# Attention output moved out of the score banks into spare columns of the turned probabilities' banks

## The chip, the cores and the metric

The kernel runs on one core of one Trainium2 chip. The metric is the device time of one execution in microseconds. Before the change it is 995.27 us, the median of three runs (992.34 to 995.49).

## What is computed

One transformer block with adaptive layer norm, on 8 batches of 512 tokens of width 256. Cut to what matters here, with `h` the modulated layer norm of `x`:

```python
# light attention: windows of 64 tokens, each sees itself and its two neighbours, 8 heads of 64
q, k, v = split(layernorm(h) @ wqkv_l)
sim = einsum('bhnid,bhnjd->bhnij', qw * scale, kk)      # kk, vv: three windows side by side
lo = einsum('bhnij,bhnjd->bhnid', softmax(sim), vv);  light_out = lo @ wo_l
# heavy attention: 256 tokens chosen by a routing score as queries, 256 as keys
ho = einsum('bhij,bhjd->bhid', softmax(hq * scale @ hk), hv);  heavy_out.at[iq].set(ho @ wo_h)
x = x + ga * (light_out + heavy_out)
# MLP: y = square(relu(n(x) @ W_fc.T)) @ W_proj.T, then five steps of a spiking neuron on y
x = x + gb * spikes(y) / 5
```

## The kernel before

Five instruction streams are written out by hand, one for each engine (TensorE, VectorE, ScalarE, GpSimd, SyncE), and are tied together by counting semaphores. What an engine does comes in the order in which its stream issues it. There is no scheduler.

Attention is cut into 24 slots for each batch, which make one iteration: 16 light ones (`LIGHT`; a pair of heads p and a tile of 128 queries m) and 8 heavy ones. There are 8 iterations: `first`, six of `loop`, and `last`. The running number of a slot is n. The work of three slots lies side by side in each slot:

- TensorE, slot n: `scores(n + 2)`, the units of the slot (projections, MLP, transposes, listed in `SLOT_UNITS`), `turn(n)` (transposes the probabilities into `ps_pT`), `attend(n - 1)` (the products with v, into `ps_oT`).
- VectorE, slot n: `copy_out(n - 2)` (adds the two parts of the output and stores them in `loT` or `hoT`, the latter inside `late`), `invert(n + 1)` (reciprocal of the row sums), `minimum(n + 2)` (row minimum of the scores), then its part of the units and of the stages (layer norm, router comparisons, neuron).
- ScalarE, slot n: `copy_pT(n - 1)` (copies the turned probabilities to `probsT`), `exp_step(n + 2)`, its part of the units, `normalize(n + 1)`.

Scores hold negative products, so the minimum is what softmax needs as maximum. The scores lie in two PSUM banks (`ps_scores`, at most 256 of 512 columns each), and the output of attention lies in columns 256 to 383 of the same two banks. The turned probabilities lie in two others (`ps_turned`, columns 0 to 255). Columns 256 to 511 of those are unused. The other four banks hold the MLP's sums and the units' results. No two engines may touch one bank at a time, so each stream waits by bank:

- `scores(n + 1)` waits for `exp_ready` of slot n.
- `attend(n - 1)` waits for `copy_pT(n - 1)`, for `copy_out(n - 2)` and for `exp_step(n + 2)`, for the latter with `pe.wait_ge(exp_ready, min(n + 4, SLOTS * B))` (L1062; its n is the slot attended to).
- `copy_out(n - 2)` waits for the end of `attend(n - 2)` and for the end of `scores(n + 2)` (L1321).
- `turn(n)` waits for `normalize(n)` and for `copy_pT(n - 1)`.

Units named below: HT (slots 0 and 2) transposes routed rows, which ScalarE and VectorE store as `hT`; V (slot 0), HV (slots 3, 7), NV (slots 20, 22, 23) are value projections, copied by VectorE; HO (slot 1) multiplies the last heavy outputs with `wo_heavy`, and waits for the copy_out of the last heavy slot, done in slot 1; Z3 (slot 7) transposes the third norm; FC and YA (slots 8 to 16) are the MLP; ZT (slots 15, 16) and RK (slots 13, 16) are a transpose (drained by ScalarE as `full`) and the ranks from the router comparisons; HQ and HK of slot 17 project routed queries and keys; LO (slots 18 to 21) is the light output projection.

Of the kernel before, what the change touches and what calls it, by code (L numbers as in the profile page):

```python
# [33 lines left out]
P = 128  # L34
B, N, D = 8, 512, 256
H, DH = 8, 64
INNER = H * DH
W = 64
SEL = 256
# [11 lines left out]
SLOTS = LIGHT + HEAVY  # L51
# [130 lines left out]
def score_columns(s, part):  # L182

    if s >= LIGHT:
        return 0, SEL
    m = s % T
    return (W if m == 0 and part == 0 else 0), (2 * W if m == T - 1 and part == 1 else 3 * W)
# [9 lines left out]
def probs_buffer(s):  # L197

    return s % T if s < LIGHT else (1, 2, T)[(s - LIGHT) % 3]


def adaln_block_kernel(nc, x, gamma_h, wq_h, wkv_h, wo_h, ln_g, ln_b, wqkv_l, wo_l, rt_q, rt_kv,
                       w_fc, w_proj, c, wmod, out):
    with ExitStack() as ctx:
        def sb(name, shape, dt=F32):
            return ctx.enter_context(nc.sbuf_tensor(name, shape, dt))

        def sem(name):
            return ctx.enter_context(nc.semaphore(name))
# [48 lines left out]
        v = sb("v", [P, T, INNER])  # L258
        v_r = sb("v_r", [P, SEL // P, INNER])
# [47 lines left out]
        gates_sign = probsT[0:B, :]  # L307

        ps_scores = ctx.enter_context(nc.psum_tensor("ps_scores", [P, 2, 512], F32))
        ps_oT = ps_scores[:, :, SEL:SEL + P]  # L310
        ps_turned = ctx.enter_context(nc.psum_tensor("ps_turned", [P, 2, 512], F32))
        ps_pT = ps_turned[:, :, 0:SEL]
        ps_y = [ctx.enter_context(nc.psum_tensor(f"ps_y{i}", [P, 512], F32)) for i in range(2)]
        ps_unit = [ctx.enter_context(nc.psum_tensor(f"ps_unit{i}", [P, 512], F32)) for i in range(BANKS)]

# [23 lines left out]
        scores_ready = sem("scores_ready")  # L339
        min_ready = sem("min_ready")  # L340
        exp_ready = sem("exp_ready")
# [3 lines left out]
        pT_copied = sem("pT_copied")  # L345
        oT_ready = sem("oT_ready")
        oT_copied = sem("oT_copied")
# [48 lines left out]
        def wait_drained(eng, segment, b, *units):  # L396

            last = {}
            for u in sorted(units, key=BANKED[segment].index):
                bank, before = bank_use(segment, b, u)  # L400
                last[bank] = before + 1
            for bank, count in last.items():
                eng.wait_ge(drained[bank], count)
# [478 lines left out]
        def _(pe):  # L882
# [160 lines left out]
            def turn(n, s):  # L1043


                pe.wait_ge(probs_ready, n + 1)
                if not (isinstance(n, int) and n == 0):
                    pe.wait_ge(pT_copied, n)
                for i in range(3 if s < LIGHT else 4):
                    for c in range(2):  # L1050
                        run = (i - 1) % 3 if s < LIGHT else i ^ 2 * c
                        rows = slice(c * W, (c + 1) * W)
                        ins = pe.transpose(ps_pT[:, c, i * W:(i + 1) * W],  # L1053
                                           probs[rows, probs_buffer(s), run * P:(run + 1) * P], ident[rows, rows])
                ins.then_inc(pT_ready, 1)

            def attend(segment, b, n, s):

                pe.wait_ge(pT_copied, n + 1)
                if n > 0:  # L1060
                    pe.wait_ge(oT_copied, n)
                pe.wait_ge(exp_ready, min(n + 4, SLOTS * B))  # L1062

                halves = [slice(i * W, (i + 1) * W) for i in range(2)]
                if s < LIGHT:
                    p, m = divmod(s, T)
                    if p == 0 and m == 2:
                        wait_drained(pe, segment, b, ("V", 3))
                    turned = probsT[:, 0:6 * W].rearrange("p (i c n) -> p i c n", i=3, c=2)
                    cols = [slice(p * P + h * DH, p * P + (h + 1) * DH) for h in range(2)]  # L1070
                    for g, h in ((0, 0), (1, 1), (1, 0), (0, 1)):
                        both = probsT[halves[g], h * W:h * W + 2 * (3 - 2 * h) * W].rearrange(
                            "p (w n) -> p w n", w=2)[:, :, 0:W]
                        ins = pe.matmul(ps_oT[halves[h], g ^ h, :], v[halves[g], m, cols[h]], both,  # L1074
                                        start=True, stop=m == (T - 1, 0)[g])
                    for g, h in ((0, 0), (1, 1), (1, 0), (0, 1)):
                        if m != (T - 1, 0)[g]:
                            w = 1 - g
                            ins = pe.matmul(ps_oT[halves[h], g ^ h, w * W:(w + 1) * W], v[halves[g], m + 1 - 2 * g, cols[h]],  # L1079
                                            turned[halves[g], 2, h ^ w, :], start=False, stop=True)  # L1080
                else:
                    p, _ = divmod(s - LIGHT, SEL // P)
                    if s == LIGHT:
                        wait_drained(pe, segment, b, ("HV", 0), ("HV", 1))
                    turned = probsT[:, :].rearrange("p (c i n) -> p i c n", c=2, i=4)
                    cols = [slice(p * P + h * DH, p * P + (h + 1) * DH) for h in range(2)]
                    for t in range(2):
                        for g, h in ((0, 0), (1, 1), (1, 0), (0, 1)):
                            ins = pe.matmul(ps_oT[halves[h], g ^ h, :], v_r[halves[g], t, cols[h]],  # L1089
                                            turned[halves[g], 2 * h + t, :, :], start=(t == 0), stop=(t == 1))  # L1090
                ins.then_inc(oT_ready, 1)

# [18 lines left out]
            for k in range(KD):  # L1111
                ins = pe.transpose(ps[:, k * B:(k + 1) * B], silu[:, 2, k * P:(k + 1) * P], ident[0:B, 0:B])
# [4 lines left out]
            for k in range(KD):  # L1117
                ins = pe.matmul(ps[:, :], silu_first[:, k, :], raw_wmod[k][:, 0:512], start=(k == 0), stop=(k == KD - 1))
# [3 lines left out]
            for q in range(4):  # L1122
                for k in range(KD):
                    ins = pe.matmul(ps[:, q * B:(q + 1) * B], raw_wmod[k][:, 3 * D + q * P:3 * D + (q + 1) * P],
                                    siluT[:, k, :], start=(k == 0), stop=(k == KD - 1))
            ins.then_inc(full_bank, 1)
            for i in range(3):
                ps, full_bank = fill("setup", 0, ("MR", i))
                for k in range(KD):
                    ins = pe.matmul(ps[0:B, :], siluT[:, k, :], raw_wmod[k][:, i * 512:(i + 1) * 512],  # L1130
                                    start=(k == 0), stop=(k == KD - 1))
# [19 lines left out]
        def _(dve):  # L1151
# [150 lines left out]
            def minimum(n, s):  # L1302
                dve.wait_ge(scores_ready, n + 1)
                (lo, hi), other = score_columns(s, 0), score_columns(s, 1)
                if (lo, hi) == other:
                    ins = dve.tensor_reduce(row_min[:, s % 3, :], ps_scores[:, :, lo:hi], AX.X, ALU.min)  # L1306
                else:
                    dve.tensor_reduce(row_min[:, s % 3, 0:1], ps_scores[:, 0, lo:hi], AX.X, ALU.min)
                    lo, hi = other
                    ins = dve.tensor_reduce(row_min[:, s % 3, 1:2], ps_scores[:, 1, lo:hi], AX.X,  # L1310
                                            ALU.min)
                ins.then_inc(min_ready, 1)
# [5 lines left out]
            def copy_out(n, s):  # L1318

                dve.wait_ge(oT_ready, n + 1)  # L1320
                dve.wait_ge(scores_ready, min(n + 5, SLOTS * B))  # L1321
                dst, (p, m) = (loT, divmod(s, T)) if s < LIGHT else (hoT, divmod(s - LIGHT, SEL // P))
                dve.tensor_reduce(dst[:, p, m * P:(m + 1) * P], ps_oT.rearrange("p g n -> p n g"), AX.X,  # L1323
                                  ALU.add).then_inc(oT_copied, 1)
# [79 lines left out]
            def iteration(segment, b, first=False, last=False):  # L1404
                for s in range(SLOTS):
                    n = SLOTS * b + s
                    if first and s in (2, 3):
                        routed_weights(s - 2)
                    if not (first and s < 2):
                        copy_out(n - 2, (s - 2) % SLOTS)  # L1410
                    if not (last and s + 1 >= SLOTS):
                        invert(n + 1, (s + 1) % SLOTS)
                    if not (last and s + 2 >= SLOTS):
                        minimum(n + 2, (s + 2) % SLOTS)
                    if not last and s == 7:
                        stats2(b + 1)
                    for u in slot_units(s, first, last):
                        unit(segment, b, u)
                    stages(segment, b, s, first, last)
# [29 lines left out]
            cols = ps[:, 0:4 * B].rearrange("p (q b) -> p q b", q=4)  # L1449
# [40 lines left out]
            for b in range(1, B - 1):  # L1490
                iteration("loop", b)
# [47 lines left out]
```

## Time and profile before

| | |
|---|---|
| median of the runs | 995.27 us (992.34 to 995.49) |
| profiled execution, its own time | 1000.88 us |
| its span | 999.1 us |
| TensorE busy | 855.5 us, 86% |
| TensorE weight loads busy | 654.3 us, 65% |
| VectorE busy | 556.6 us, 56% |
| ScalarE busy | 583.5 us, 58% |
| GpSimd busy | 396.5 us, 40% |
| mean granted TensorE clock | 0.93 |
| chain that ended last | TensorE 59%, VectorE 22%, ScalarE 8%, issue 6% |

The rows come from the profiled execution, the median from runs without a profile. Busy shares are means over the whole span; an engine may be the limit in one stretch and idle in another. Times in rows are us from the span's start. One loop iteration lasts about 112.5 us. The one read closest starts at about 501.9. The granted clock is given as a share of TensorE's full 2.4 GHz.

### The profile page before, as it was taken

The page shows a single profiled execution, that of the slowest core. Times are in us where ns is not written, and L with a number is a line of the kernel's source. Part 1 is how long each engine was busy: PE and PEld are TensorE (multiplying, and loading weights), DVE is VectorE, ACT ScalarE, POOL GpSimd, SP SyncE. Part 2 cuts the span into 40 slices and gives each one's busy share as a digit, 9 for nine tenths or more (in the row PEclk, how much of TensorE's full clock was granted, in tenths as well). Part 3 has the DMA queues.
Part 4 walks back from the last instruction along what each step waited for, and adds up shares of the span by engine and source line. Part 5 has one row for each costly group of instructions (what it writes and reads, how often), then busy time and mean ns, then how long its engine had stood idle before and what let it go on. Part 6 is the DMA issues. An engine that isn't in the chain of part 4 may idle for free.

```text
span 999.1 us, 23412 instructions
## 1 busy us (share of the span) xinstructions
PE 855.5 (86%) x8914; PEld 654.3 (65%) x8914; DVE 556.6 (56%) x1602; ACT 583.5 (58%) x1682; POOL 396.5 (40%) x437
## 2 busy tenths in 40 slices
PE   5758599799988999799988999799988999899655
PEld 2436466577756876577756876577756876587455
DVE  7645634764557554764557554764557554614344
ACT  1156556576656765676656765576556765676332
POOL 3322031375424542365424543365424542252243
PEclk9878779999999999999999999999999999999768
DMA  8220002100210012200220012200220011200100
GB/s 314 67 80 2 27 28 70 59 2 23 80 59 23 2 38 85 59 2 19 71 73 23 1 39 85 60 2 17 72 73 22 3 38 54 59 2 2 37 22 22
DMA packets 32479, 45.33 MB, mean 45 GB/s; under 512 B 3928, under 2 KB 26720, under 8 KB 32368
## 3 DMA queue, kind: packets, MB, share of 16 engines
q1 hardware_dynamic: 26944, 31.24, 9.8%
q0 software_dynamic: 4608, 12.59, 3.8%
q8 instruction: 72, 1.18, 0.5%
q14 instruction: 39, 0.32, 0.1%
q10 hardware_dynamic: 816, 0.00, 0.0%
HBM read 28.85 MB, written 14.97 MB: 44 GB/s over the span
## 4 chain that ended last, share of the span: by engine, by line
PE 59%; DVE 22%; ACT 8%; issue 6%; DMA 2%; POOL 2%; SPq 0%; DVEq 0%; POOLq 0%; ACTq 0%
PE ps_unit L895 25%; PE ps_y L1006 7%; PE ps_unit L943 6%; ACT probs L829 5%; PE ps_unit L948 4%; PE ps_turned L1053 4%; PE ps_scores L1089 3%; PE ps_scores L1074 3%; DVE row_min L1306 3%; PE ps_scores L1038 3%; PE ps_scores L1029 3%; DVE loT L1323 2%; ACT hT L794 1%; DVE bn L1268 1%; DMA late<-in_L_wmod 1%
## 5 line engine op out<-in xcount | busy, mean ns | idle before, releaser
L829 ACT ACTIVATE probs<-ps_scores,row_min 128x192 f32<-128x192 f32 (+2 forms) x384 | 161.3, 425 | 182.8 <-DVE row_min L1306 125.6
L839 ACT ACTIVATE probs<-probs,row_inv 128x192 f32<-128x192 f32 (+2 forms) x384 | 155.7, 458 | 0.0
L1323 DVE TENSOR_REDUCE loT<-ps_scores 128x128 f32<-128x256 f32 x128 | 53.5, 418 | 141.3 <-PE ps_scores L1029 92.0
L895 PE MATMUL ps_unit<-xT,wfcT 128*128 128x512 f32 (+1 forms) x432 | 112.8, 404 | 9.4 <-DVE xT L1247 8.8
L895 PE MATMUL ps_unit<-xT,wqkv 128*128 128x512 f32 x384 | 109.6, 422 | 3.3 <-POOL xT L653 3.3
L1006 PEld LDWEIGHTS ps_y<-wprojT,hid_parts 128*128 128x128 f32 x768 | 99.3, 190 | 9.9 <-issue 6.0
L432 POOL TENSOR_TENSOR hid<-hid 128x512 f32<-128x512 f32 (+1 forms) x64 | 63.5, 992 | 106.4 <-ACT hid L807 105.1
L1006 PE MATMUL ps_y<-wprojT,hid_parts 128*128 128x256 f32 x768 | 104.6, 284 | 0.2
L895 PEld LDWEIGHTS ps_unit<-xT,wfcT 128*128 128x128 f32 x432 | 78.6, 206 | 33.4 <-issue 20.2
L578 POOL TENSOR_SCALAR veps<-mv 128x4 f32<-128x4 f32 (+1 forms) x25 | 5.1, 202 | 227.7 <-DVE mv L1166 133.1
L1074 PE MATMUL ps_scores<-probsT,v 64*64 64x128 f32 x1024 | 58.7, 299 | 38.9 <-ACT probs L829 38.6
L1053 PEld LDWEIGHTS ps_turned<-ident,probs 64*128 64x128 f32 x1280 | 55.6, 140 | 54.9 <-issue 44.3
L895 PEld LDWEIGHTS ps_unit<-xT,wqkv 128*128 128x128 f32 x384 | 71.3, 193 | 24.3 <-issue 10.2
L436 POOL TENSOR_TENSOR hid_parts<-hid,hid_parts 128x512 fp32r<-128x512 f32 (+1 forms) x64 | 79.2, 1237 | 13.4 <-ACT hid_parts L811 11.2
L1053 PE MATMUL ps_turned<-ident,probs 64*128 64x64 f32 x1280 | 82.2, 241 | 1.9 <-ACT probsT L851 1.7
L619 POOL DMA_INDIRECT sorted_rows<-hn,rank x64 | 64.4, 1006 | 45.7 <-DVE rank L1350 33.0
L847 ACT ACTIVATE probsT<-ps_turned 128x384 f32<-128x384 f32 x128 | 61.9, 484 | 33.6 <-PE ps_scores L1079 33.3
L1306 DVE TENSOR_REDUCE row_min<-ps_scores 128x2 f32<-128x512 f32 (+1 forms) x128 | 77.1, 602 | 2.5 <-PE ps_scores L1029 2.5
L1323 DVE TENSOR_REDUCE late<-ps_scores 128x128 f32<-128x256 f32 x64 | 27.0, 422 | 88.0 <-PE ps_scores L1038 44.8
L829 ACT ACTIVATION_READ_ACCUMULATOR probs<-ps_scores,row_min 128x1 f32 x384 | 75.3, 196 | 0.0
L1029 PE MATMUL ps_scores<-kT,qT 64*64 64x192 f32 (+1 forms) x1024 | 71.8, 317 | 3.3 <-ACT probs L829 3.3
L943 PE MATMUL ps_unit<-wo_light,loT 128*128 128x256 f32 x256 | 63.8, 392 | 0.0
(158 smaller groups left out, 1690.9 us busy)
## 6 DMA issues: line engine op xcount, KB each, us to landing
xa<-in_L_attn_x SPq DMA_DIRECT2D x8, 512.0 KB, 5.0
routed<-sorted_rows SPq DMA_DIRECT2D x16, 256.0 KB, 3.0
lx<-in_L_attn_x SPq DMA_DIRECT2D x8, 512.0 KB, 3.8
out_x<-spikes SPq DMA_DIRECT2D x16, 256.0 KB, 3.0
routed_out<-late SPq DMA_DIRECT2D x8, 256.0 KB, 2.1
full<-mod_rows SPq DMA_DIRECT2D x7, 256.0 KB, 5.0
sorted_rows<-hn,rank POOLq DMA_INDIRECT x64, 2.4
gate_a<-mod_rows SPq DMA_DIRECT2D x8, 128.0 KB, 3.5
```

What stands on the lines that cost most here:

```text
L436: eng.tensor_tensor(hid_parts[1][:, i % 2, cols], square, hid_parts[0][:, i % 2, cols].bitcast(F32), ALU.subtract).then_inc(low, 1)
L619: pool.indirect_dma_start(out=sorted_rows[r], out_offset=bass.IndirectOffsetOnAxis(ap=rank[:, r, t:t + 1], axis=0), in_=hn[:, t, :], in_of ...
L829: ins = act.activation(probs[:, probs_buffer(s), probs_columns(s, part)], ps_scores[:, part, lo:hi], ACT.Exp, bias=row_min[:, s % 3, part: ...
L839: ins = act.activation(rows, rows, ACT.Identity, scale=row_inv[:, s % 3, part:part + 1])
L895: ins = pe.matmul(ps, w(wi, k, w_cols), a(ai, k, a_cols), start=(n == 0), stop=(n == 3 * KD - 1))
L943: ins = pe.matmul(ps[:, 0:D], loT[:, p, i * P:(i + 1) * P], wo_light[:, p, :], start=(p == 0), stop=(p == PAIRS - 1))
L1006: ins = pe.matmul(ps_y[t // 2][:, (t % 2) * D:(t % 2 + 1) * D], hid_parts[hi][:, i % 2, t * P:(t + 1) * P], wprojT[wi][:, f, :], start=(f ...
L1029: ins = pe.matmul(ps_scores[c * W:(c + 1) * W, w, lo:hi], qT[heads[h], p % 2, query:query + W], kT[heads[h], p % 2, first_key + lo:first_k ...
L1053: ins = pe.transpose(ps_pT[:, c, i * W:(i + 1) * W], probs[rows, probs_buffer(s), run * P:(run + 1) * P], ident[rows, rows])
L1074: ins = pe.matmul(ps_oT[halves[h], g ^ h, :], v[halves[g], m, cols[h]], both, start=True, stop=m == (T - 1, 0)[g])
L1306: ins = dve.tensor_reduce(row_min[:, s % 3, :], ps_scores[:, :, lo:hi], AX.X, ALU.min)
L1323: dve.tensor_reduce(dst[:, p, m * P:(m + 1) * P], ps_oT.rearrange("p g n -> p n g"), AX.X, ALU.add).then_inc(oT_copied, 1)
```

## The change

The output tile `ps_oT` moves from `ps_scores` to the spare columns of `ps_turned`. Since turn writes bank c from the row half c, the products of the output now go to the bank of their row half g, in place of g ^ h. attend no longer waits for the exponential. turn waits for the copy_out of two slots before, whose bank it writes. copy_out waits for the copy of the turned probabilities, which reads the same banks, in place of the scores, and VectorE issues it behind the inverse and the minimum instead of ahead of them.

```diff
-        ps_oT = ps_scores[:, :, SEL:SEL + P]
         ps_turned = ctx.enter_context(nc.psum_tensor("ps_turned", [P, 2, 512], F32))
         ps_pT = ps_turned[:, :, 0:SEL]
+        ps_oT = ps_turned[:, :, SEL:SEL + P]
...
                 pe.wait_ge(probs_ready, n + 1)
-                if not (isinstance(n, int) and n == 0):
+                if n > 0:
                     pe.wait_ge(pT_copied, n)
+                if n > 1:
+                    pe.wait_ge(oT_copied, n - 1)
...
                 pe.wait_ge(pT_copied, n + 1)
                 if n > 0:
                     pe.wait_ge(oT_copied, n)
-                pe.wait_ge(exp_ready, min(n + 4, SLOTS * B))
...
-                        ins = pe.matmul(ps_oT[halves[h], g ^ h, :], v[halves[g], m, cols[h]], both,
+                        ins = pe.matmul(ps_oT[halves[h], g, :], v[halves[g], m, cols[h]], both,
                                         start=True, stop=m == (T - 1, 0)[g])
...
-                            ins = pe.matmul(ps_oT[halves[h], g ^ h, w * W:(w + 1) * W], v[halves[g], m + 1 - 2 * g, cols[h]],
+                            ins = pe.matmul(ps_oT[halves[h], g, w * W:(w + 1) * W], v[halves[g], m + 1 - 2 * g, cols[h]],
...
-                            ins = pe.matmul(ps_oT[halves[h], g ^ h, :], v_r[halves[g], t, cols[h]],
+                            ins = pe.matmul(ps_oT[halves[h], g, :], v_r[halves[g], t, cols[h]],
...
                 dve.wait_ge(oT_ready, n + 1)
-                dve.wait_ge(scores_ready, min(n + 5, SLOTS * B))
+                dve.wait_ge(pT_copied, min(n + 2, SLOTS * B))
...
-                    if not (first and s < 2):
-                        copy_out(n - 2, (s - 2) % SLOTS)
                     if not (last and s + 1 >= SLOTS):
                         invert(n + 1, (s + 1) % SLOTS)
                     if not (last and s + 2 >= SLOTS):
                         minimum(n + 2, (s + 2) % SLOTS)
+                    if not (first and s < 2):
+                        copy_out(n - 2, (s - 2) % SLOTS)
```

## Rows read from the trace of the kernel before

**Rows 1.** Waits of the whole span: who waited for whom, total us, times, longest us.
```profile
ACT probs L829 <- DVE row_min L1306: 125.6, 128, 2.8
ACT probs L829 <- DVE row_min L1310: 57.1, 57, 2.7
PE ps_scores L1074 <- ACT probs L829: 38.6, 47, 2.1
```
**Rows 2.** Timeline, slot 4: start, length, engine, line, operation, idle time before and its releaser.
```profile
522.35 0.41 DVE L1323 TENSOR_REDUCE loT<-ps_scores 128x128 f32<-128x256 f32 x1
522.68 0.15 DVE L1316 RECIPROCAL row_inv<-row_sum 128x2 f32<-128x2 f32 x1
522.75 0.53 DVE L1306 TENSOR_REDUCE row_min<-ps_scores 128x2 f32<-128x384 f32 x1
...
522.89 0.40 PE L1053 MATMUL ps_turned<-ident,probs 64*128 64x64 f32 x6
523.21 1.66 DVE L1186 SCALAR_TENSOR_TENSOR h<-xa,rstd,full 128x256 f32<-128x256 f32 x4
...
524.38 0.45 PE L1074 MATMUL ps_scores<-probsT,v 64*64 64x128 f32 x8 [1.09 <-ACT probs L829]
```
**Rows 3.** Timeline of TensorE, slot 7: an output and the scores behind it.
```profile
536.69 0.45 PE L1074 MATMUL ps_scores<-probsT,v 64*64 64x128 f32 x8
...
537.07 0.51 PE L1029 MATMUL ps_scores<-kT,qT 64*64 64x192 f32 x8
```
**Rows 4.** Timeline, slot 1: the copy of the last heavy output, and HO.
```profile
506.74 0.42 DVE L1323 TENSOR_REDUCE late<-ps_scores 128x128 f32<-128x256 f32 x1
...
507.30 5.38 PE L948 MATMUL ps_unit<-wo_heavy,late 128*128 128x256 f32 x16 [1.59 <-DVE late L1323]
```
**Rows 5.** Timeline, slot 23: copy, turn, and the heavy output.
```profile
612.04 0.42 DVE L1323 TENSOR_REDUCE late<-ps_scores 128x128 f32<-128x256 f32 x1 [2.12 <-PE ps_scores L1029]
...
613.43 0.46 PE L1053 MATMUL ps_turned<-ident,probs 64*128 64x64 f32 x8
...
614.09 0.67 PE L1089 MATMUL ps_scores<-probsT,v_r 64*64 64x128 f32 x16 [0.19 <-ACT probs L829]
```
**Rows 6.** Timelines of TensorE and VectorE: HV in slot 3, the copy in slot 5.
```profile
518.47 1.66 PE L895 MATMUL ps_unit<-wkv_r,hT 128*128 128x512 f32 x6 [0.72 <-DVE hT L1342]
```
```profile
525.40 0.42 DVE L1323 TENSOR_REDUCE loT<-ps_scores 128x128 f32<-128x256 f32 x1 [0.53 <-PE ps_scores L1029]
```
**Rows 7.** Timelines, slots 15 and 16: cast, copy, RK and output.
```profile
576.59 0.43 DVE L1244 CAST xT<-full 128x512 fp32r<-128x512 f32 x1 [1.75 <-ACT full L764]
...
579.42 0.41 DVE L1323 TENSOR_REDUCE loT<-ps_scores 128x128 f32<-128x256 f32 x1
```
```profile
579.64 0.24 PE L980 MATMUL ps_unit<-ones_bf,late 128*128 128x1 bf16 x4 [0.55 <-DVE late L1234]
...
581.69 0.45 PE L1074 MATMUL ps_scores<-probsT,v 64*64 64x128 f32 x8 [1.02 <-ACT probs L829]
```
**Rows 8.** Waits inside the first iteration, then inside the last one.
```profile
PE ps_scores L1074 <- ACT probs L829: 10.9, 12, 2.1
```
```profile
PE ps_scores L1074 <- ACT probs L829: 2.4, 5, 1.1
...
PE ps_scores L1089 <- ACT probs L829: 1.6, 2, 0.8
```
**Rows 9.** Stretches: bounds, length, busy us of PE, PEld, DVE, ACT, POOL, clock, DMA.
```profile
528.00:532.00 4.00, 2.89 (x43) 1.88 (x36) 3.06 (x14) 2.48 (x10) 1.23 (x2) 1.00 0.38 131
578.50:582.50 4.00, 2.43 (x54) 1.82 (x52) 2.24 (x8) 1.97 (x6) 1.05 (x1) 1.00 0.09 33
582.60:586.00 3.40, 3.40 (x19) 3.39 (x17) 2.51 (x7) 2.33 (x8) 2.70 (x3) 0.51 0.08 25
```
**Rows 10.** Timeline of TensorE: HO and FC of iteration 1, FC of iteration 4.
```profile
172.45 3.69 PE L948 MATMUL ps_unit<-wo_heavy,late 128*128 128x256 f32 x16 [1.57 <-DVE late L1323]
...
202.03 3.03 PE L895 MATMUL ps_unit<-xT,wfcT 128*128 128x512 f32 x12 [1.00 <-DVE xT L1247]
...
538.58 4.44 PE L895 MATMUL ps_unit<-xT,wfcT 128*128 128x512 f32 x12 [1.00 <-DVE xT L1247]
```

## Prediction

> **What bounds the kernel now.** I read the page first. TensorE is busy for 86% of the span, VectorE for 56%, ScalarE for 58%, and two thirds of the chain that ended last is TensorE's. So time can only come from TensorE's idle time, or from TensorE running at the wrong clock.
>
> The list of waits comes second [rows 1]. ScalarE's exponentials wait for the row minimum 128 + 57 times, that is in practically every slot, about 1 us each. The exponential therefore starts when the minimum ends, not when ScalarE comes free. TensorE's largest single wait is the one in front of the attention output: 38.6 us in 47 places, all for the exponential. It is the line `pe.wait_ge(exp_ready, min(n + 4, ...))` in attend, there because the output lies in the score banks that the exponential is still reading. Heavy slots wait little.
>
> Third I read one slot in order of time [rows 2]. It is slot 4. VectorE comes free late at F = 522.35 (its centering of the next batch ran until then), copies the output of two slots ago (L1323), and only then takes the minimum (start 522.75, next VectorE instruction 523.21). TensorE has finished turning the probabilities (522.89 + 0.40 = 523.29) and stands for 1.09 us until the attention output can start at 524.38. The scores of the next slot come 0.38 us behind such an output [rows 3].
>
> Last I read the granted clock in stretches. It is 1.00 nearly everywhere in the loop, except for three stretches of about 3.4 us in nearly every loop iteration at about half, the lower level of 1.2 GHz: in HO (slot 1), in the first FC units (slot 8) and in HQ/HK (slot 17).
>
> **The change, part by part.** TensorE's operations, their number and their order stay; so do VectorE's but for copy_out, which goes from before the inverse and the minimum to behind them. No DMA moves, and SP's and POOL's queues are untouched. A wait in attend (for the exponential) goes, one in turn (for copy_out) comes, copy_out waits for the copy of the turned probabilities instead of the scores.
>
> *(a) The minimum no longer stands behind the copy.* L1323 delays the next VectorE instruction by 0.33 us (start to start, 522.35 to 522.68, where the inverse begins [rows 2]). Minimum, exponential and all that ScalarE does behind it come 0.33 us earlier where ScalarE waits for the minimum, which is nearly always [rows 1].
>
> *(b) The output no longer waits for the exponential.* The next wait is that of the next scores, which still need the exponential. The output's 0.38 us [rows 3] go under that wait. (a) and (b) together can give 0.33 + 0.38 = 0.71 us per long wait, and a short wait whole.
>
> *(c) The new wait.* turn now waits for copy_out, which stands behind inverse and minimum. From F: 0.07 (inverse) + 0.46 (minimum, 522.75 to 523.21) + 0.42 (copy) + about 0.12 hand-over. The last is an estimate from [rows 4], where the copy ends at 507.16 and TensorE's HO follows at 507.30. So turn starts no earlier than F + 1.07, output F + 1.47, next scores F + 1.85. Behind turn on TensorE's queue stand the output and these scores. Before, the scores came at 524.38 + 0.38 = F + 2.41. A slot with a long wait thus gives 0.56 us, a slot with a short one (w below 0.56) gives w. In slots without a wait the copy is in time. The tightest one that I found is slot 23 [rows 5]: copy ready at 612.04 + 1.07 = 613.11, turn at 613.43, 0.32 us spare. From below (the copy takes turn's whole gain) a slot gives 0, from above 0.71.
>
> *(d) Slot by slot through one loop iteration* (waits for the exponential in slots 2, 4, 5, 6, 16, 23).
> Slot 23: the wait of 0.19 goes [rows 5]: 0.18.
> Slot 1: HO needs the copy of the last heavy output [rows 4]. The copy comes 0.53 later behind inverse and minimum. The chain before it (exponential of slot 0, hT, the copy of V) comes 0.33 earlier. That costs 0.20 us, hidden by nothing: TensorE stands for 1.59 us already.
> Slots 2 and 3: HV waits for hT, which ScalarE makes behind the exponential [rows 6]: 0.33 earlier, by (a), whatever attend does.
> Slots 4 to 8: slot 4 would give 0.56. But VectorE sat idle only 0.53 before slot 5's copy [rows 6]; from there to FC in slot 8 it works nearly without a stop, so slots 5 and 6 pass nothing more on (FC waits for its last product). 0.53.
> Slots 15 and 16: RK waits 0.55 for the comparisons, these for a cast, this for ScalarE's `full` behind the exponential [rows 7]: 0.33 earlier. Then slot 16's own 0.71, less a few hundredths because turn waits for the copy: 0.67.
> Sum 0.18 - 0.20 + 0.33 + 0.53 + 1.00 = 1.84 us per iteration, 11.0 us in the six loop iterations. The first iteration has 12 waits with 10.9 us [rows 8], nine of them over 0.56: at most 5.6 us; I take 4, since some of these slots are paced by VectorE's weight parts. The last one has 4.0 us in 7 waits [rows 8] and the HO loss; capped at 0.56 each I take 2.5. Waits: 17.5 us.
>
> *(e) The clock.* In the 4 us before HQ, TensorE was busy for 2.43 us at full clock, then the clock fell for 3.4 us [rows 9]. In a like stretch around slot 6 it was busy for 2.89 us and the clock stayed. The change takes 1.0 us of idle time out of exactly the first stretch, and leaves it busier than the second. I expect this fall to go, six times. Price of one: HO took 5.38 us with one [rows 4] and 3.69 without [rows 10], 1.69; FC 4.44 against 3.03 [rows 10], 1.41; in HQ, 3.40 us all busy at 0.51 are 1.67 us lost [rows 9]. I take 1.6, so 9.5 us. The falls in HO and FC stand behind waits that the change doesn't shorten; I leave them in, and put their going in the range.
>
> By the Trainium skill (TensorE: Matmul & The Clock Gate, Part 1) the clock falls after an idle stretch and comes back after a busy one. Here it fell after stretches that were mostly busy by the trace, so the trace agrees in direction only. Read as idle alone, no wait of 1 us would matter, no fall would go, and the sum would be that of the second rival.
>
> *(f) Banks of the output's products.* The output now goes to bank g (the half of the rows that are contracted) instead of g ^ h. Sixteen heavy records of 128 columns take 0.67 us [rows 5], 0.042 each; a whole-array record of 256 columns takes 3.69/16 = 0.231 [rows 10], 0.115 for 128. Two to three run at a time already, two row halves on one bank included. I take 0; bounds are 0 and half the output's time, -0.19 us in each of 192 slots, -36 us.
>
> The Trainium skill (TensorEngine Tiling (Array Packing), Restrictions and Gotchas) says that different row tiles can't access the same bank at once. If they were held apart now, the new placing would free them, which gives the fourth rival. The overlap just worked out speaks against it.
>
> **Sum.** Against the profiled execution's own 1000.88 us: 1000.88 - 17.5 - 9.5 = 973.9, a ratio of 0.973. The median of the runs is 995.27, so 968.4 us.
>
> **Rivals.**
> 1. *More falls of the clock go.* With each iteration shorter, HO and FC meet other states of the clock; the second iteration already shows HO at 3.69 and FC at 3.03. All would give 6 x 1.69 + 5 x 1.41 = 17.2 more: 956.7, or 951.3 at the median. Against it: the waits before HO and FC remain. 0.22, mostly part of it.
> 2. *Only the waits go; HQ's fall stays.* 1000.88 - 17.5 = 983.4, at the median 977.9. For it: 2.43 and 2.89 of 4 us lie near one another. 0.17.
> 3. *turn takes over the wait.* If the hand-over from minimum to copy to turn costs 0.5 us more than I take, (c) gives nothing, and only the 0.33 of HV and of RK remain: about 4 us, 991. 0.06. For it: in slot 4 the new wait is 0.53 us, near to what it replaces.
> 4. *The output's products run faster.* Up to 36 us beyond the forecast; half of that gives 950. 0.03.
> 5. *Slower: new falls.* Slots 2 to 7 run at full clock now, with four waits. Idle time there moves together, to in front of turn (0.5 us) and of the scores. If this makes the clock fall, each fall costs 1.6 us. It decides from 17 falls on (27/1.6), three in each iteration; two in each together with HQ's fall staying make it even. At four in each it is about 1007 (24 x 1.6 = 38.4 lost against 27.0 gained). 0.06.
> The forecast itself has 0.42, and 0.04 is left for what I don't see.
>
> **Numbers.** 968.4 us. Its own range is 962 to 974. The whole range goes up to rival 2 with some weakening (982) and down to nearly all falls gone (952). This leaves rivals 3 to 5 and the rest outside, about 0.19. A difference under 0.3% (3 us) can't be told from no change. Faster by more: 0.42 + 0.22 + 0.17 + 0.03 and two thirds of rival 3, 0.88. Within 0.3%: 0.05. Slower: 0.07.
>
> **What the profile after would show.** The wait of the output for the exponential is gone from the list of waits. In its place stand the scores' wait for the exponential, and turn's for loT/late, in slots 4, 6 and 16, together about half of the old 41 us. The exponential starts about 0.1 us after the minimum as now, but 0.33 us earlier behind the scores. HO's wait is about 1.8 us instead of 1.59. The clock is 1.00 in the HQ units, 12 of them in 1.69 us. An iteration of the loop takes about 3.4 us less. The forecast is wrong if turn's wait sums to more than 20 us, if the HQ units still take 2.9 us (too low by 9), or if HO and FC run at full clock (too high by up to 17).

## The result and the profile after

The changed kernel takes 967.97 us (median of four executions, 965.52 to 968.22) against 995.38 us. The ratio is 0.971, 95% interval 0.966 to 0.976. In the profiled execution the span is 966.3 us where it was 999.1. The profiled execution of before lay 5.5 us above its median, so of these 32.8 us some five are chance. The spread of executions below goes largely, but not wholly, with the granted clock. Ratios leave out an execution that lies over 1.5% above the shortest one of its kernel; here that is one of the first experiment's six.

The list of waits of the changed kernel (total us, times, longest us; answers to [rows 1] and, for HO, to [rows 4]):

```profile
ACT probs L829 <- DVE row_min L1307: 79.0, 99, 2.5
...
ACT probs L829 <- DVE row_min L1311: 34.9, 27, 2.5
...
PE ps_turned L1055 <- DVE loT L1324: 18.6, 28, 1.4
...
PE ps_unit L948 <- DVE late L1324: 12.2, 8, 1.7
...
DVE late L1324 <- ACT probsT L851: 6.4, 3, 2.7
DVE loT L1324 <- ACT probsT L847: 6.2, 15, 0.7
...
PE ps_scores L1029 <- ACT probs L829: 3.7, 3, 1.7
...
PE ps_turned L1055 <- DVE late L1324: 3.4, 4, 1.5
```

The output's wait for the exponential (38.6 us) is gone. turn's wait for the copy has come, 22.0 us. ScalarE's wait for the minimum went from 182.7 to 113.9 us: the minimum comes earlier. VectorE has a new wait of its own, for ScalarE's copy of the turned probabilities (12.6 us).

Slot 4 of the iteration whose HO starts at 491.98, in order of time (answers to [rows 2]):

```profile
505.01 0.15 DVE L1317 RECIPROCAL row_inv<-row_sum 128x2 f32<-128x2 f32 x1
505.09 0.53 DVE L1307 TENSOR_REDUCE row_min<-ps_scores 128x2 f32<-128x384 f32 x1
505.54 0.41 DVE L1324 TENSOR_REDUCE loT<-ps_turned 128x128 f32<-128x256 f32 x1
...
506.10 0.40 PE L1055 MATMUL ps_turned<-ident,probs 64*128 64x64 f32 x6 [0.57 <-DVE loT L1324]
506.43 0.45 PE L1075 MATMUL ps_turned<-probsT,v 64*64 64x128 f32 x8
```

VectorE comes free at F = 505.01. The copy ends at 505.95, turn starts at F + 1.09 (forecast F + 1.07), the output at F + 1.42, where it was F + 2.03.

One iteration, by three marks on TensorE: HO in slot 1, HV in slot 3, FC in slot 8, and the next HO. Before they stood at 507.30, 518.47 [rows 6], 538.58 [rows 10] and 619.89.

```profile
491.98 3.69 PE L948 MATMUL ps_unit<-wo_heavy,late 128*128 128x256 f32 x16 [1.64 <-DVE late L1324]
501.12 1.66 PE L895 MATMUL ps_unit<-wkv_r,hT 128*128 128x512 f32 x6 [0.96 <-DVE hT L1343]
...
520.87 4.44 PE L895 MATMUL ps_unit<-xT,wfcT 128*128 128x512 f32 x12 [1.00 <-DVE xT L1248]
...
561.90 0.24 PE L980 MATMUL ps_unit<-ones_bf,late 128*128 128x1 bf16 x4 [0.58 <-DVE late L1235]
...
562.90 0.46 PE L1055 MATMUL ps_turned<-ident,probs 64*128 64x64 f32 x8 [0.35 <-DVE loT L1324]
...
564.21 1.70 PE L895 MATMUL ps_unit<-hT,wq_r 128*128 128x256 f32 x12
```

The next HO starts at 599.85. The iteration lasts 107.87 us; it was 112.59. From HO to HV it gained 2.03 us, of which 1.69 is HO at full clock (3.69 us, was 5.38) and 0.34 the waits. From HV to FC it gained 0.36. From FC to the next HO it gained 2.33, of which 1.51 is HQ and HK at full clock (from the first HQ to turn it was 4.58 us, 582.61 to 587.19, and is 3.07, 564.21 to 567.28) and 0.82 the waits. So the waits gave 1.52 us and the clock 3.20. FC ran at the lower level in both.

Stretches of the changed kernel (columns as in [rows 9]): around slot 6, before HQ, HQ itself, HO, FC.

```profile
510.00:514.00 4.00, 2.94 (x38) 2.00 (x38) 3.06 (x14) 2.33 (x9) 1.23 (x2) 1.00 0.44 135
560.60:564.60 4.00, 3.07 (x58) 2.35 (x57) 2.58 (x10) 2.15 (x7) 1.20 (x2) 1.00 0.11 37
564.20:567.60 3.40, 3.40 (x35) 3.26 (x32) 2.91 (x8) 2.89 (x9) 2.38 (x3) 1.00 0.00 0
...
492.00:495.40 3.40, 3.40 (x16) 2.91 (x16) 0.42 (x1) 1.08 (x5) 0.00 (x0) 1.00 0.00 0
520.90:524.30 3.40, 3.40 (x9) 2.69 (x10) 2.14 (x11) 1.40 (x5) 0.72 (x1) 0.55 0.01 2
```

Before HQ, TensorE is now busy for 3.07 of 4 us (was 2.43), and the clock stays at 1.00. I counted the falls to 1.2 GHz between the first and the last HO of the loop, from the granted clock in stretches of 1 us; one fall is 3.4 us. Before there were 16 (five in HO, five in FC, six in HQ). After there are 7, one of them in HO, none in HQ, the others around Z3 and FC.

The iteration from the first HO of the loop to the second separates the two shares, since each kernel has one fall in it: 109.49 us with one in HQ before, 108.15 us with one in HO after. Less that fall (1.51 and 1.69) they are 107.98 and 106.46 us, and the difference is the same 1.52 us. Falls around Z3 cost less than others: iterations of the changed kernel whose only fall begins there last 107.18 and 107.08 us, 0.6 to 0.7 more than 106.46.

### The profile page after: what moved, and what is told of

It is laid out like the page before. It is cut to its first block, busy times and chain, and to the rows that moved or that the text cites. A ratio compares the mean times of both kernels' runs of the same rounds, so it can differ in the third digit from the quotient of the medians.

```text
span 966.3 us, 23395 instructions
## 1 busy us (share of the span) xinstructions
PE 838.0 (87%) x8914; PEld 640.2 (66%) x8914; DVE 571.9 (59%) x1602; ACT 586.2 (61%) x1682; POOL 399.5 (41%) x437
## 4 chain that ended last, share of the span: by engine, by line
PE 63%; DVE 19%; ACT 6%; issue 6%; DMA 2%; POOL 2%; SPq 0%; DVEq 0%; POOLq 0%; ACTq 0%
PE ps_unit L895 27%; PE ps_y L1006 9%; PE ps_unit L943 6%; PE ps_turned L1055 5%; PE ps_turned L1090 3%; PE ps_unit L948 3%; PE ps_turned L1075 3%; PE ps_scores L1038 3%; PE ps_scores L1029 2%; ACT probs L829 2%; DVE row_min L1307 2%; DVE hT L1343 1%; ACT hT L794 1%; DVE bn L1269 1%; DMA late<-in_L_wmod 1%
## 5 line engine op out<-in xcount | busy, mean ns | idle before, releaser
L1055 PE MATMUL ps_turned<-ident,probs 64*128 64x64 f32 x1280 | 82.9, 241 | 22.9 <-DVE loT L1324 18.6
L811 ACT ACTIVATE hid_parts<-hid 128x512 fp32r<-128x512 f32 (+1 forms) x72 | 42.1, 584 | 40.7 <-PE ps_y L1006 40.2
L1309 DVE TENSOR_REDUCE row_min<-ps_scores 128x1 f32<-128x128 f32 x64 | 20.1, 314 | 68.5 <-PE ps_scores L1029 68.4
L1075 PE MATMUL ps_turned<-probsT,v 64*64 64x128 f32 x1024 | 59.7, 305 | 0.0
```

Of the source, the lines that this page charges most:

```text
L1055: ins = pe.transpose(ps_pT[:, c, i * W:(i + 1) * W], probs[rows, probs_buffer(s), run * P:(run + 1) * P], ident[rows, rows])
L1075: ins = pe.matmul(ps_oT[halves[h], g, :], v[halves[g], m, cols[h]], both, start=True, stop=m == (T - 1, 0)[g])
```

## The experiments

Falls below are always counted in this way, in the profiled execution of each kernel.

**The wait for the exponential put back (e1).** The change without its gain in attend:

```diff
                 if n > 0:
                     pe.wait_ge(oT_copied, n)
+                pe.wait_ge(exp_ready, min(n + 4, SLOTS * B))
```

> The changed kernel with one line put back: attend waits for the exponential again, although nothing in the banks needs it any more. The output stays in the spare columns, copy_out stays behind the minimum. Theory (both halves count: the earlier minimum and the output out of the exponential's way): from F, the moment at which VectorE comes free, the scores come at F + 2.08 instead of F + 1.85 in slots with a long wait (F + 2.41 in the kernel before), and HV and HO are as in the changed kernel. That loses about 0.5 us per iteration, 4 us in all, and as much again if falls of the clock before HQ come back: 972 to 982 us. Rival (the wait for the exponential was the whole cost, the order of VectorE nothing): nearly all of the gain goes, 988 us or more. In the trace TensorE's wait for the exponential in front of the output should be about half of the 38.6 us of before.

Measured: 984.56 us as the median of all six executions, 981.94 without the longest of them. The ratio to before, which leaves that one out, is 0.984 (0.979 to 0.988). This lies between the two kernels, at the upper end of the theory's range (with the falls before HQ back), and below the rival's 988. The waits in its trace, and the slots before HQ with the clock:

```profile
PE ps_turned L1055 <- DVE loT L1325: 17.6, 27, 1.2
...
PE ps_turned L1076 <- ACT probs L829: 8.2, 33, 1.1
```
```profile
570.90:574.90 4.00, 2.81 (x56) 2.43 (x57) 2.67 (x7) 1.63 (x6) 1.71 (x2) 1.00 0.11 37
575.20:578.60 3.40, 3.40 (x21) 3.25 (x17) 2.76 (x8) 2.60 (x8) 2.56 (x3) 0.57 0.02 8
```

turn's wait is as in the changed kernel. The wait for the exponential is 8.2 us, less than half of 38.6, since most of it now lies under turn's. But the clock falls before HQ are back in all six iterations, and there are 14 falls instead of 7. So the line costs little as a wait (8.2 us in the whole span, while the loop is 16.1 us longer than in the changed kernel), and the larger part of its price comes with the falls of the clock that return with it. The six executions spread from 974.65 to 989.76 us, in the order of their granted clock (0.958, 0.949, 0.942, 0.936, 0.933, 0.933).

**VectorE's old order (e2).** The change in banks and waits, but the copy ahead of the minimum:

```diff
+                    if not (first and s < 2):
+                        copy_out(n - 2, (s - 2) % SLOTS)
                     if not (last and s + 1 >= SLOTS):
                         invert(n + 1, (s + 1) % SLOTS)
                     if not (last and s + 2 >= SLOTS):
                         minimum(n + 2, (s + 2) % SLOTS)
-                    if not (first and s < 2):
-                        copy_out(n - 2, (s - 2) % SLOTS)
```

> The changed kernel with VectorE's old order: copy_out ahead of the inverse and the minimum. The output stays in the spare columns and attend does not wait for the exponential. Theory: the minimum is 0.33 us later than in the changed kernel, so the scores come at F + 2.03 (F + 1.85 in the changed kernel), HV is 0.33 later, and HO is as in the kernel before (1.59 us of wait instead of 1.65). Per iteration that gives 0.18 + 0.38 + 0.38 = 0.9 us instead of 1.5: 4 us slower than the changed kernel, 972 us with the same falls of the clock, up to 980 with more of them. turn's wait for the copy (18.6 us in the changed kernel) should be near zero, and the scores should wait for the exponential in its place. Rival (turn's new wait is what holds the changed kernel, so taking it away helps): faster than the changed kernel, 960 us or less.

Measured: 1012.81 us, ratio 1.015 (1.012 to 1.018). Slower than the kernel before, and neither theory had it. Its waits, and one slot in which TensorE doesn't wait (a packed slot):

```profile
DVE loT L1324 <- ACT probsT L847: 175.9, 84, 6.3
ACT probs L829 <- DVE row_min L1307: 163.4, 124, 2.8
...
DVE late L1324 <- ACT probsT L851: 107.0, 48, 4.7
```
```profile
554.45 0.47 ACT L847 ACTIVATE probsT<-ps_turned 128x384 f32<-128x384 f32 x1
555.02 0.42 DVE L1324 TENSOR_REDUCE loT<-ps_turned 128x128 f32<-128x256 f32 x1 [2.07 <-ACT probsT L847]
555.36 0.15 DVE L1317 RECIPROCAL row_inv<-row_sum 128x2 f32<-128x2 f32 x1
555.43 0.27 DVE L1309 TENSOR_REDUCE row_min<-ps_scores 128x1 f32<-128x128 f32 x1
...
556.00 0.37 ACT L829 ACTIVATE probs<-ps_scores,row_min 128x128 f32<-128x128 f32 x1 [1.08 <-DVE row_min L1311]
```

In the banks of the turned probabilities the copy must wait until ScalarE has copied these, in 132 of 192 slots. That copy ends at 554.92 here, while the scores' first records stand at 553.66. So copy, minimum and exponential come one after another behind ScalarE, and the minimum starts about 1.8 us behind the scores (555.43 against 553.66; in a slot of the kind of the next two, 579.38 against 577.54). In the kernel before it was 1.17 (574.17 against 573.00), in the changed one 0.68 (556.00 against 555.32). The clock isn't the reason: this kernel has 14 falls where the one before has 16. turn's wait for `loT` is 9.9 us, not near zero, and the scores wait 15.3 us for the exponential, which was expected. I had costed the new wait of copy_out only where VectorE comes late. In the new banks the old order loses. The new order in the old banks wasn't run: there the copy and the exponential both read the score banks, so the exponential would have to wait for the copy as before. That is argued and not shown.

**The products' banks alone.** Putting the output's products on bank g while it lies in the score banks wasn't tried: there the scores of the other row half would write the same bank right behind, with nothing between them. The traces with the output in the other banks show no price: its records take 0.45 and 0.67 us before and after, and the next scores follow a light output at 0.38 in both (503.43 against 503.05 after).

**TensorE kept busy (e4 before, e5 changed).** Products that nobody needs, into a bank that is overwritten next, in TensorE's waits of the six loop iterations and the last one; once in the kernel before, once in the changed one:

```diff
+            def keep_busy(bank, count):
+                for _ in range(count):
+                    pe.matmul(bank[:, :], wqkv[0][:, 0, 0:P], wqkv[0][:, 0, 0:512], start=True, stop=True)
...
+                if segment in ("loop", "last") and u == ("Z3", 1):
+                    pe.wait_ge(y_free, 2 * b)
+                    keep_busy(ps_y[0], 6)
                 ps, full_bank = fill(segment, b, u)
+                if segment in ("loop", "last") and u in BUSY:   # HO(0): 6, FC(0): 4, RK(1): 2
+                    keep_busy(ps, BUSY[u])
```

> The kernel before with products that nobody needs in TensorE's idle time: 6 of 512 columns in front of HO(0), 6 in front of Z3(1), 4 in front of FC(0), 2 in front of RK(1). They fill waits and change nothing else. Theory (a part of the time is TensorE's clock, which falls after stretches with waits): HO and FC run at full clock in all iterations, 11 falls of 1.41 to 1.69 us go, 978 us; if those in front of HQ go too, 969. Rival (the clock in these units has another cause, or the falls move on to other work): the time stays at 995 or rises by the cost of the products, and the stretches of 1.2 GHz are as many as before.

> The changed kernel with the same products in front of HO(0), Z3(1), FC(0) and RK(1). Theory: the seven falls of the clock that the loop of the changed kernel still has go, 7 x 1.6 = 11 us: 957 to 960 us. The difference to the kernel before with the same products is then the waits alone where neither falls: 1.5 us in each of six loop iterations and some 6 us in the first and the last, 15 us, plus 9 us if HQ still falls in the kernel before. Rival (the gain of the change was mostly clock): the two kernels with the products lie within 8 us of one another.

Measured: 989.22 us (ratio 0.992, 0.990 to 0.995) for the kernel before, 962.62 us (0.966, 0.963 to 0.969) for the changed one. The falls in the loop went from 16 to 1 and from 7 to none (one more stands 13 us behind the kernel before's last HO), so the clock does depend on what TensorE does in these waits. Both times are longer than expected (978 or 969, and 957 to 960): they gained less than the clock, since the products also stand in the way. The kernel before with them, in slots 16 and 17:

```profile
570.47 0.71 PE L902 MATMUL ps_unit<-wqkv 128*128 128x512 f32 x2
571.75 0.46 PE L1063 MATMUL ps_turned<-ident,probs 64*128 64x64 f32 x8
573.31 0.45 PE L1084 MATMUL ps_scores<-probsT,v 64*64 64x128 f32 x8 [1.09 <-ACT probs L830]
...
574.23 1.69 PE L896 MATMUL ps_unit<-hT,wq_r 128*128 128x256 f32 x12
```

Two products stand in RK's wait, 0.7 us together. The output still waits 1.09 us for the exponential, and HQ runs at full clock in five of six iterations, 1.69 us for what took 2.93. That these two did it isn't shown, since those in front of HO, Z3 and FC came with them. Loop iterations without a fall last about 109.5 us in the one and 107.2 us in the other, 2.2 us apart. Without products it was 107.98 and 106.46. So the products cost 1.5 us an iteration in the kernel before and 0.8 in the changed one, and of the 2.2 us 1.5 are the waits of the change, as in the accounting above, and 0.7 is the products' own.

The two medians lie 26.6 us apart, where 15 were expected and the rival (the gain is mostly clock) had at most 8, so the rival falls. By the two profiles, which lie 25.8 us apart, 14.9 come in the six loop iterations (six times 2.2 and one fall). The products don't reach the first iteration and what is ahead of it: there the two differ by 7.1 us (first HO at 171.48 and 164.35), in waits and clock, which no run separates. The remaining 3.8 us stand behind the last HO.

**The same kernel again, and HO's copy first.** Four kernels on one chip: the changed kernel itself as the measure (e9), HO's copy first (e6), fewer products (e8), and both of these (e7).

> The changed kernel itself once more, as the measure for the three others on the same chip. 966 to 970 us. If the spread between executions is the clock's, executions with a higher granted clock are the shorter ones, as with e1.

Measured: 973.55 us (970.37 to 978.26), ratio 0.977 (0.972 to 0.982). The same program was 5.6 us slower than in its first measurement. The profile has the same waits within 0.1 us in HO (12.2 us) and Z3 (13.1), though turn's wait for `loT` is 24.0 us instead of 18.6. It has 11 falls in the loop instead of 7: four iterations have two falls in a row around Z3 and FC, and last 109.1 to 109.4 us. The loop is 7.4 us longer than in the first profile, while the first HO comes 3.8 us earlier. Six executions go from 970.37 at a clock of 0.954 to 978.26 at 0.944. Between the two measurements the mean clock says nothing, though: the first had 0.941 to 0.949 with the shorter times. It is a mean over the whole span, and time at the lower level doesn't cost the same everywhere (0.6 us for a fall around Z3, 1.69 for one in HO).

```diff
+                    if s == 1 and not first:
+                        copy_out(n - 2, (s - 2) % SLOTS)
                     ... invert, minimum ...
-                    if not (first and s < 2):
+                    if s != 1 and not (first and s < 2):
                         copy_out(n - 2, (s - 2) % SLOTS)
```

> The changed kernel, but in slot 1 of each iteration copy_out goes ahead of inverse and minimum again, since HO waits for just this copy. Theory: in slot 1 VectorE comes late from the copy of V (0.7 us after the turned probabilities are copied), so the copy waits for nothing; HO starts 0.46 us earlier, its wait is 1.2 us instead of 1.65, and the exponential, 0.33 later, is hidden behind the 3.7 us of HO. Seven iterations give 3.2 us: 965 us, or 3 us less than the changed kernel on this chip. Rival (HO's start does not matter, VectorE's norm statistics behind it set the next slot): no difference.

Measured: 973.46 us against 973.55, which is the rival's range. HO's wait did what was expected, and the time didn't:

```profile
PE ps_unit L948 <- DVE late L1324: 8.6, 8, 1.1
```

3.6 us of wait went. The profile has 12 falls in the loop, all six iterations with two in a row. FC in the second loop iteration, first of the changed kernel measured again, then of this one:

```profile
305.12 4.58 PE L895 MATMUL ps_unit<-xT,wfcT 128*128 128x512 f32 x12
```
```profile
302.90 5.46 PE L895 MATMUL ps_unit<-xT,wfcT 128*128 128x512 f32 x12 [0.93 <-DVE xT L1248]
```

Counted from HO (275.12 and 273.44) FC starts 0.54 us earlier here, but more of it runs at the lower level, and it takes 0.88 us longer. The iteration lasts 109.03 us against 109.12. So what HO's earlier start gave was lost again at the clock behind it, in these iterations at least.

> e5 with fewer idle products: 4 in front of HO(0), 5 in front of Z3(1), 2 in front of FC(0), none in front of RK(1). Theory: e5's products in front of FC and RK ran longer than the waits they fill (the third of the kernel's time that was won at the clock, 9 us, showed only as 5), so with fewer the clock stays up and less is in the way: 958 to 961 us. Rival (so few no longer hold the clock): falls come back and the time lies between e5 and the changed kernel, 963 to 967.

> e6 and e8 together, with 3 products in front of HO(0), whose wait is shorter. Theory: both gains add, since one is a wait and the other the clock: 3 us below e8, 955 to 958 us. Rival (they are the same gain): as e8.

With fewer products (`BUSY = {("HO", 0): 4, ("FC", 0): 2}` and 5 for Z3) the changed kernel takes 963.29 us, 1 fall in the loop. With HO's copy first and 3 products in HO as well it takes 960.87 us (ratio to before 0.963, 0.959 to 0.968), 2 falls. The first is as e5 within their spread, so fewer products gave nothing more, and 963.29 lies in the rival's range. The second is above the 955 to 958 us that were expected, but 2.4 us below the first. Without a fall, loop iterations last about 107.0 us in the first and 106.45 in the second: with the clock held up, HO's earlier start shows as 0.5 us an iteration, near the 3 us that were expected. All three of these falls are HQ's. Here are the 4 us before HQ of the first of the two kernels, in an iteration that stayed at full clock and in one that fell, and both HQ:

```profile
447.88:451.88 4.00, 3.06 (x59) 2.34 (x57) 2.57 (x8) 1.76 (x6) 1.59 (x2) 1.00 0.09 33
554.80:558.80 4.00, 3.07 (x59) 2.34 (x57) 2.57 (x8) 1.76 (x6) 1.59 (x2) 1.00 0.09 33
```
```profile
451.88 1.69 PE L896 MATMUL ps_unit<-hT,wq_r 128*128 128x256 f32 x12
```
```profile
558.80 2.57 PE L896 MATMUL ps_unit<-hT,wq_r 128*128 128x256 f32 x12
```

The work ahead is the same on every engine, and one HQ falls and the other doesn't. It is also as busy as in the changed kernel (3.07), where none of the six fell. The last kernel is the fastest here, 12.7 us below the changed kernel on the same chip.

## Why the prediction held

The forecast was 968.4 us, the median is 967.97. That it is this near is luck in part: the same program measured again has 973.55. By its steps:

- *(a), (c).* Right. Scores to minimum is shorter by 0.49 us in packed slots. turn starts at F + 1.09 in slot 4 against F + 1.07 (the hand-over is 0.15 us; in [rows 4] too it is 0.14, where I took 0.12), and the tight slot 23 has no wait.
- *(b).* Right in that the output's wait goes. I expected the scores to wait for the exponential in its place. They don't (3.7 us in three places, 3.3 before): turn's wait covers it. In slot 4 the exponential's records end at 506.57, and the scores stand at 506.70.
- *(d).* 1.52 us an iteration where I had 1.84. Slots 2 and 3 gave 0.34 (0.33). Slots 4 to 8 gave 0.36 where I had 0.53: in slot 5 the copy waits 0.16 us for ScalarE's copy of the turned probabilities (first line below), in the middle of VectorE's unbroken work, and all behind it moves. That wait stands in the change, and I had not costed it there. From FC to HO it was 0.82 where I had 0.98 (1.00 + 0.18 - 0.20). RK gave nothing: its wait is 0.58, was 0.55, because ScalarE's `full`, once the exponential came earlier, waited 0.29 us for ZT on TensorE (second line). HO lost less than the 0.20, its wait is 1.64 to 1.66.

```profile
508.22 0.42 DVE L1324 TENSOR_REDUCE loT<-ps_turned 128x128 f32<-128x256 f32 x1 [0.16 <-ACT probsT L847]
...
558.04 0.78 ACT L764 ACTIVATE full<-ps_unit,ln_cols 128x512 f32<-128x512 f32 x1 [0.29 <-PE ps_unit L953]
```

- *(e).* The outcome came: HQ's falls went in all six iterations, worth 9.1 us (forecast 9.5). They come back with the wait for the exponential (e1), and five of six go from the kernel before with the unneeded products (e4). The argument for it was weaker than it looked. I compared the busy shares 2.43 and 2.89 of 4 us, and such a share doesn't settle it: HQ stayed at full clock in four of six iterations with 2.58 (e2), and fell with 3.07 in one of six (e8). I left the falls in HO and FC in. The five in HO went besides, and one new came, which was the first rival in part, though HO's own wait didn't shrink. In the second measurement the falls around Z3 and FC were more.
- *(f).* Nothing, as taken: the records take 0.45 and 0.67 us with either placing.

Against its own profiled execution the loop gained 25.6 us: 9.1 by the waits (forecast 11.0) and about 16.5 by the clock (forecast 9.5; the 7 us more are nearly all HO's). Up to the first HO the gain was 3.7 us, behind the last one 3.4, of which 1.69 is HO's clock. The near hit at the median thus has two misses of opposite sign in it, and an execution before that lay 5.5 us above its median. The second rival (waits only) was wrong. The third (turn takes over the wait) was right by half: turn waits for 22.0 us, where the output waited for 41.5. I had named more than 20 us there as a sign of being wrong, and it came. The waits did give less than forecast (1.52 against 1.84), while the forecast of the time held. One reading of the page was too high: TensorE has 59% of the chain that ended last, not two thirds.

Open: what decides in which iterations HO, FC and HQ fall. The runs show that it changes between measurements of one program and between iterations with the same work ahead, and that work in the waits makes the falls rarer (from 16 to 1, from 7 to none), no more.

## What to carry to other kernels

When a tile moves to another bank, cost both new partners of that bank in every slot, not only in those with a wait: here the move with VectorE's old order made the kernel 1.5% slower, and with the copy behind the minimum it was 2.3% to 2.9% faster. Where TensorE's waits lie close together, look at the granted clock behind them; a fall cost 0.6 to 1.7 us there. Measure such a kernel by several executions with their clock. To compare the waits alone, take iterations with no fall, or with one whose price is known. Unneeded products hold the clock up, but cost time of their own, and not the same in both versions.

## What the runs showed of the hardware

How busy TensorE was in the 4 us before HQ, and in how many of the six loop iterations HQ then ran at 1.2 GHz:

| kernel | busy, us of 4 | HQ at 1.2 GHz |
|---|---|---|
| before | 2.43 to 2.44 | 6 of 6 |
| VectorE's old order (e2) | 2.58 to 2.59 | 2 of 6 |
| wait put back (e1) | 2.81 | 6 of 6 |
| before, with products (e4) | 2.91 | 1 of 6 |
| changed, both measurements, and e6 | 3.06 to 3.07 | 0 of 6 each |
| changed, fewer products (e8, e7) | 3.06 to 3.07 | 1 and 2 of 6 |
| changed, more products (e5) | 3.54 to 3.55 | 0 of 6 |

By and large falls are rarer with more work ahead, but the share doesn't tell the cases apart: with 2.58 four of six stayed, with 2.81 none did, and with 3.07 three of twelve fell once the kernel had the products. In front of HO the same holds inside one execution of e1, where the first stretch stayed at full clock behind it and the second fell (HO 3.69 and 5.38 us):

```profile
386.71:390.71 4.00, 2.35 (x35) 1.50 (x34) 2.40 (x8) 3.03 (x12) 0.00 (x0) 1.00 0.00 0
496.51:500.51 4.00, 2.36 (x36) 1.50 (x34) 2.40 (x8) 3.03 (x12) 0.00 (x0) 1.00 0.02 4
```

The unneeded products, whose results nobody reads, brought the falls down. One program had medians of 967.97 and 973.55 us in two measurements, with equal waits in HO and Z3 and 7 against 11 falls.
